# Another order of the steps in a talking-heads attention kernel with a local-attention gate

## The reference

```
s = talking_heads_attention(xn)      # 16 heads of 16; heads mixed before and after the softmax
g = silu(local_attention_stack(xn))  # 2 layers: window attention (8 heads of 64) and a GELU MLP
return x + s * g
```

## Time and profile before

| | |
|---|---|
| median of 3 runs | 5370.03 us (5368.29 to 5371.4) |
| the profiled execution, its own time | 5372.07 us |
| its span, first to last instruction | 5370.0 us |
| mean granted TensorE clock | 0.994 of full speed |
| busy: TensorE / VectorE / ScalarE / GpSimd | 95% / 69% / 50% / 49% |
| DMA | 52 GB/s over the span |

### The profile page before, as it was taken

How to read it: one execution, slowest core, us unless ns; L and a number is a source line. 1 busy time by engine, 2 the same in 40 slices (tenths; PEclk the granted TensorE clock), 3 DMA queues, 4 the chain that set the end, 5 groups by cost and what they waited for, 6 DMA issues and landing times. The chain is left out here.

```text
span 5370.0 us, 176617 instructions
## 1 busy us (share of the span) xinstructions
PE 5119.1 (95%) x72856; PEld 4155.2 (77%) x72856; DVE 3692.1 (69%) x8889; ACT 2659.8 (50%) x6551; POOL 2619.2 (49%) x2308
## 2 busy tenths in 40 slices
PE   6999999999999999999999999999999999999998
PEld 5887777877778777787777777777777777777776
DVE  6667676667766667666676666766667676676765
ACT  4445554455544454544545445454455544555544
POOL 4445554445544445444464444544445444454543
PEclk9999999999999999999999999999999999999999
DMA  2211111121111111111110111101111011111110
GB/s 79 95 66 63 46 35 64 45 67 42 38 61 56 57 41 38 61 61 53 40 64 35 61 53 51 58 31 61 54 50 58 30 61 62 42 58 39 52 49 17
DMA packets 51388, 280.78 MB, mean 52 GB/s; under 512 B 5280, under 2 KB 22688, under 8 KB 33696
## 3 DMA queue, kind: packets, MB, share of 16 engines
q1 hardware_dynamic: 39840, 252.69, 12.8%
q0 software_dynamic: 10752, 16.78, 1.7%
HBM read 249.01 MB, written 28.84 MB: 52 GB/s over the span
## 5 line engine op out<-in xcount | busy, mean ns | idle before, releaser
L1492 POOL TENSOR_TENSOR q_lo<-q_mix,q_hi 128x512 fp32r<-128x512 f32 x512 | 663.5, 1296 | 1349.7 <-ACT q_hi L979 1349.7
L992 ACT ACTIVATE probs<-bank_S,neg_max 128x512 f32<-128x512 f32 x1024 | 700.6, 685 | 1180.3 <-DVE neg_max L1220 993.7
L711 PE MATMUL bank_S<-k_hi,q_lo 128*128 128x512 f32 x2048 | 874.5, 427 | 9.6 <-POOL q_lo L1492 5.5
L1220 DVE TENSOR_REDUCE neg_max<-bank_S 128x1 f32<-128x512 f32 x1024 | 693.8, 684 | 263.5 <-PE bank_S L713 259.7
L713 PE MATMUL bank_S<-k_hi,q_hi 128*128 128x512 f32 x2048 | 803.9, 393 | 0.0
L712 PE MATMUL bank_S<-k_lo,q_hi 128*128 128x512 f32 x2048 | 803.5, 392 | 0.1
L728 PEld LDWEIGHTS bank_M<-mixer_n,probs 64*64 64x64 f32 x32768 | 534.1, 136 | 248.5 <-issue 161.3
L728 PE MATMUL bank_M<-mixer_n,probs 64*64 64x64 f32 x32768 | 606.1, 222 | 74.3 <-DVE mixer_n L1211 24.3
L1518 POOL TENSOR_TENSOR l_probs<-l_probs,l_inv 128x1024 f32<-128x1024 f32 (+1 forms) x256 | 428.8, 1682 | 491.7 <-DVE l_inv L1323 491.7
L1487 POOL TENSOR_TENSOR q_mix<-q_rope,w_pre 128x256 f32<-128x256 f32 x1024 | 637.6, 643 | 48.6 <-POOL q_lo L1492 1.8
L1042 ACT ACTIVATE l_probs<-l_probs,l_least 128x256 f32<-128x256 f32 (+1 forms) x1024 | 480.9, 471 | 253.0 <-DVE l_least L1303 252.6
...
## 6 DMA issues: line engine op xcount, KB each, us to landing
...
```

The source lines that it names most:

```text
L711: mm(bank[k][:], q_lo[q], k_hi[:, s, :], start=(s == 0), stop=False)
L992: fn(probs[:, n % PB, :], bank[k][:], ACT.Exp, bias=neg_max[:, n % 2:n % 2 + 1], accum_out=row_sum[:, n % 4:n % 4 + 1]).then_inc(emptied[k ...
L1220: v.tensor_reduce(neg_max[:, n % 2:n % 2 + 1], bank[k][:], AX.X, ALU.max, negate=True)\
L1492: g.tensor_tensor(q_lo[:, c % QB], q_mix[:], q_hi[:, c % QB].bitcast(F32), ALU.subtract)\
```

## The change

It replaces ORDER and LAST_ORDER by other permutations of the same steps, and swaps two neighbours in FIRST_ORDER. No step, instruction, buffer or DMA is added or removed. Two waits are added so that the new order is safe: talk_v on TensorE waits until both banks of x_turn.0 are taken out, and ScalarE's x_turn waits for all three talk projections to be filled. The number of times that consecutive TensorE steps use different tile shapes, counted over the whole of `program()` from the texts, is 1904 before and 1914 after. Of the two large texts, the lines that the next sections speak of:

```diff
 ORDER = """
...
-q_turn.0.1 qkv.0.3 part.4 mix.1 scores.5 q_turn.0.2 join.0.3 mixers.2 k_turn.0.2 scores.6 scores.7 expand.5 mix.2
-sigmoid.0 part.5 mixers.3 q_turn.0.3 k_turn.0.3 scores.8 scores.9 mix.3 local_scores.0.0 mixers.4 expand.6 part.6
-expand.7 sigmoid.1 weigh.0.0 values.0 local_scores.0.1 mix.4 part.7 expand.8 scores.10 scores.11 weigh.0.1 p_turn.0.0
-local_scores.0.2 part.8 mixers.5 expand.9 scores.12 scores.13 mix.5 local_scores.0.3 local_values.0.0 weigh.0.2
-mixers.6 scores.14 scores.15 mix.6 weigh.0.3 p_turn.0.1 sigmoid.2 part.9 silu scores.16 gated sigmoid.3 mixers.7
-p_turn.0.2 local_values.0.1 local_scores.0.4 expand.10 scores.17 scores.18 out_proj.0.0 mix.7 part.10 local_scores.0.5
-weigh.0.4 p_turn.0.3 local_values.0.2 values.1 mixers.8 local_scores.0.6 store local_values.0.3 p_turn.0.4 weigh.0.5
-scores.19 mix.8 local_scores.0.7 expand.11 out_proj.0.1 local_values.0.4 weigh.0.6 weigh.0.7 mixers.9 p_turn.0.5
-part.11 scores.20 expand.12 local_values.0.5 p_turn.0.6 part.12 mix.9 out_proj.0.2 expand.13 local_values.0.6
...
-part.18 scores.30 scores.31 expand.19 qkv.1.0 join.1.0 scores.32 mixers.15 qkv.1.1 q_turn.1.0 k_turn.1.0 part.19
-scores.33 join.1.1 scores.34 mix.15 mixers.16 qkv.1.2 k_turn.1.1 join.1.2 values.3 scores.35 expand.20 q_turn.1.1
...
-scores.45 scores.46 mix.21 local_scores.1.4 local_values.1.1 weigh.1.3 mixers.22 part.24 p_turn.1.2 weigh.1.4
-scores.47 local_scores.1.5 mix.22 expand.25 out_proj.1.0 scores.48 weigh.1.5 mixers.23 local_values.1.2 part.25
-p_turn.1.3 mix.23 local_scores.1.6 local_values.1.3 scores.49 p_turn.1.4 expand.26 mixers.24 part.26 scores.50
...
-part.27 scores.52 local_values.1.5 p_turn.1.6 scores.53 expand.28 mixers.25 part.28 out_proj.1.2 mix.25 p_turn.1.7
...
-scale up.1.2 scores.62 scores.63 mixers.31 x_turn.0 up.1.3 up.1.4 talk_q up.1.5 mix.31 talk_k down.1.0 down.1.1
-down.1.2 talk_v values.7 down.1.3 project.3
...
+mixers.1 expand.5 k_turn.0.1 qkv.0.3 mix.1 scores.5 scores.6 join.0.3 q_turn.0.2 part.5 k_turn.0.2 q_turn.0.3 expand.6
+sigmoid.0 k_turn.0.3 mixers.2 part.6 scores.7 local_scores.0.0 mix.2 mixers.3 weigh.0.0 scores.8 scores.9 expand.7
+mix.3 part.7 local_scores.0.1 p_turn.0.0 scores.10 weigh.0.1 mixers.4 values.0 sigmoid.1 expand.8 part.8
+local_values.0.0 scores.11 local_scores.0.2 mix.4 mixers.5 expand.9 scores.12 scores.13 p_turn.0.1 weigh.0.2 mix.5
+part.9 expand.10 silu sigmoid.2 scores.14 mixers.6 scores.15 gated local_values.0.1 sigmoid.3 p_turn.0.2 mixers.7
+part.10 scores.16 mix.6 expand.11 local_scores.0.3 scores.17 out_proj.0.0 mix.7 scores.18 weigh.0.3 local_scores.0.4
+values.1 mixers.8 local_values.0.2 weigh.0.4 p_turn.0.3 local_scores.0.5 part.11 local_values.0.3 p_turn.0.4 scores.19
+weigh.0.5 mix.8 expand.12 local_scores.0.6 part.12 mixers.9 out_proj.0.1 local_values.0.4 local_scores.0.7 mix.9
+weigh.0.6 expand.13 p_turn.0.5 scores.20 scores.21 local_values.0.5 p_turn.0.6 weigh.0.7 scores.22 part.13
...
+mixers.15 expand.19 down.0.0 down.0.1 down.0.2 down.0.3 mix.15 x_turn.1 scores.33 scores.34 mixers.16 qkv.1.0 join.1.0
+qkv.1.1 values.3 join.1.1 q_turn.1.0 part.19 k_turn.1.0 expand.20 qkv.1.2 part.20 mix.16 q_turn.1.1 expand.21
...
+scores.47 expand.25 out_proj.1.0 scores.48 weigh.1.4 mix.22 local_scores.1.5 local_values.1.2 mixers.23 p_turn.1.3
+part.25 scores.49 mix.23 local_scores.1.6 local_values.1.3 mixers.24 expand.26 part.26 expand.27 values.5 weigh.1.5
...
+scores.51 scores.52 part.28 local_values.1.5 p_turn.1.6 expand.29 weigh.1.7 mixers.25 scores.53 mix.25 mixers.26
+out_proj.1.2 part.29 local_values.1.6 p_turn.1.7 expand.30 scores.54 local_values.1.7 scores.55 mix.26 mixers.27
...
+up.1.0 mix.30 up.1.1 scores.62 scores.63 mixers.31 up.1.2 up.1.3 mix.31 x_turn.0 talk_v values.7 up.1.4 up.1.5 talk_q
+talk_k down.1.0 down.1.1 down.1.2 down.1.3 project.3
 FIRST_ORDER = """
...
-part.23 scores.44 p_turn.1.2 scores.45 expand.24 mix.21 local_scores.1.5 part.24 local_values.1.2 out_proj.1.0
+part.23 p_turn.1.2 scores.44 scores.45 expand.24 mix.21 local_scores.1.5 part.24 local_values.1.2 out_proj.1.0
...
 LAST_ORDER = """
...
-mixers.28 values.6 part.31 h_scale.1 scores.59 scores.60 mix.28 mixers.29 end.silu h_turn.1 scores.61 scores.62
-mixers.30 mix.29 up.1.0 up.1.1 up.1.2 up.1.3 up.1.4 up.1.5 scores.63 mix.30 down.1.0 down.1.1 down.1.2 mixers.31
-down.1.3 end.bound mix.31 end.gated end.sigmoid.0 end.sigmoid.1 end.sigmoid.2 end.sigmoid.3 values.7 project.3
-end.store
+h_scale.1 scores.59 expand.31 mix.28 mixers.29 h_turn.1 scores.60 part.31 scores.61 mix.29 up.1.0 up.1.1 up.1.2 up.1.3
+up.1.4 up.1.5 scores.62 down.1.0 mixers.30 end.silu down.1.1 down.1.2 down.1.3 end.bound scores.63 end.gated mix.30
+end.sigmoid.0 mixers.31 end.sigmoid.1 end.store mix.31 end.sigmoid.2 end.sigmoid.3 values.7 project.3
@@ -685,6 +684,8 @@
                     last.then_inc(filled[k], 1)
 
             def talk_v(step):
+                for c in range(KC):
+                    pe.wait_ge(emptied[f"F{c}"], now.fill(("x_turn", 0), f"F{c}"))
                 for t in range(TW):
                     k = f"S{t // 2}"
                     if t % 2 == 0:
@@ -949,7 +950,8 @@
 
                 if now.past(l):
                     act.wait_ge(filled["F2"], now.fill(("qkv", (l - 1) % LAYERS, TW - 1), "F2", ago=not l))
-                    act.wait_ge(filled["S1"], now.fill(("talk_v",), "S1", ago=not l))
+                    for kind in ("talk_q", "talk_k", "talk_v"):
+                        act.wait_ge(filled["S1"], now.fill((kind,), "S1", ago=not l))
                 for c in range(KC):
                     k = f"F{c}"
                     act.wait_ge(filled[k], now.fill(step, k))
```

More of the change, by code:

```diff
@@ L140 @@
-part.18 scores.30 scores.31 expand.19 qkv.1.0 join.1.0 scores.32 mixers.15 qkv.1.1 q_turn.1.0 k_turn.1.0 part.19
-scores.33 join.1.1 scores.34 mix.15 mixers.16 qkv.1.2 k_turn.1.1 join.1.2 values.3 scores.35 expand.20 q_turn.1.1
-mix.16 mixers.17 part.20 qkv.1.3 q_turn.1.2 k_turn.1.2 project.1 expand.21 join.1.3 scores.36 part.21 scores.37 mix.17
-scores.38 q_turn.1.3 expand.22 part.22 mixers.18 k_turn.1.3 scores.39 mix.18 local_scores.1.0 mixers.19 scores.40
-scores.41 mix.19 mixers.20 local_scores.1.1 weigh.1.0 expand.23 scores.42 part.23 values.4 local_scores.1.2 p_turn.1.0
@@ L145 @@
-scores.43 expand.24 weigh.1.1 weigh.1.2 scores.44 mix.20 local_scores.1.3 mixers.21 local_values.1.0 p_turn.1.1
-scores.45 scores.46 mix.21 local_scores.1.4 local_values.1.1 weigh.1.3 mixers.22 part.24 p_turn.1.2 weigh.1.4
-scores.47 local_scores.1.5 mix.22 expand.25 out_proj.1.0 scores.48 weigh.1.5 mixers.23 local_values.1.2 part.25
-p_turn.1.3 mix.23 local_scores.1.6 local_values.1.3 scores.49 p_turn.1.4 expand.26 mixers.24 part.26 scores.50
-out_proj.1.1 local_values.1.4 expand.27 values.5 local_scores.1.7 mix.24 weigh.1.6 weigh.1.7 p_turn.1.5 scores.51
@@ L155 @@
-down.1.2 talk_v values.7 down.1.3 project.3
+expand.0 part.0 expand.1 part.1 expand.2 bound qkv.0.0 join.0.0 scores.0 scores.1 part.2 qkv.0.1 mixers.0 k_turn.0.0
+q_turn.0.0 expand.3 join.0.1 scores.2 part.3 expand.4 qkv.0.2 mix.0 scores.3 scores.4 join.0.2 part.4 q_turn.0.1
+mixers.1 expand.5 k_turn.0.1 qkv.0.3 mix.1 scores.5 scores.6 join.0.3 q_turn.0.2 part.5 k_turn.0.2 q_turn.0.3 expand.6
+sigmoid.0 k_turn.0.3 mixers.2 part.6 scores.7 local_scores.0.0 mix.2 mixers.3 weigh.0.0 scores.8 scores.9 expand.7
@@ new lines @@
+weigh.0.5 mix.8 expand.12 local_scores.0.6 part.12 mixers.9 out_proj.0.1 local_values.0.4 local_scores.0.7 mix.9
+weigh.0.6 expand.13 p_turn.0.5 scores.20 scores.21 local_values.0.5 p_turn.0.6 weigh.0.7 scores.22 part.13
+out_proj.0.2 mixers.10 local_values.0.6 store p_turn.0.7 scores.23 local_values.0.7 project.0 out_proj.0.3 expand.14
+mix.10 half_turn.0 part.14 mixers.11 scores.24 mix.11 expand.15 shift_turn.0 scores.25 scores.26 values.2 mixers.12
+part.15 expand.16 h_scale.0 scores.27 scores.28 mixers.13 mix.12 h_turn.0 part.16 expand.17 scores.29 scores.30
@@ new lines @@
+mixers.14 mix.13 up.0.0 part.17 mix.14 up.0.1 up.0.2 up.0.3 up.0.4 up.0.5 expand.18 part.18 scores.31 scores.32
+mixers.15 expand.19 down.0.0 down.0.1 down.0.2 down.0.3 mix.15 x_turn.1 scores.33 scores.34 mixers.16 qkv.1.0 join.1.0
+qkv.1.1 values.3 join.1.1 q_turn.1.0 part.19 k_turn.1.0 expand.20 qkv.1.2 part.20 mix.16 q_turn.1.1 expand.21
+scores.35 join.1.2 k_turn.1.1 qkv.1.3 q_turn.1.2 project.1 mixers.17 k_turn.1.2 scores.36 join.1.3 part.21 scores.37
+mix.17 mixers.18 q_turn.1.3 expand.22 part.22 scores.38 k_turn.1.3 scores.39 mix.18 local_scores.1.0 expand.23
@@ new lines @@
+mixers.19 weigh.1.0 scores.40 scores.41 mix.19 local_scores.1.1 mixers.20 p_turn.1.0 scores.42 weigh.1.1 values.4
+part.23 local_values.1.0 local_scores.1.2 scores.43 mix.20 weigh.1.2 local_scores.1.3 expand.24 part.24 mixers.21
+p_turn.1.1 scores.44 scores.45 mix.21 local_scores.1.4 p_turn.1.2 weigh.1.3 local_values.1.1 mixers.22 scores.46
```

(38 more changed lines are left out.)

8 lines of the change are left out of this document (removed).

## The result

The changed kernel takes 5445.6 us (median of 4 runs, 5436.0 to 5454.6) against 5370.7 us: ratio 1.014, interval 1.0122 to 1.0158. It is slower by 75 us where 57 us less were forecast, and outside the range.

A forecast was written before the change was run, and what follows sets the result against it. TensorE was taken as the bound. Idle time falls 10.4 - 7.4 = 3.0 us a batch, 45 us over batches 1 to 15; with 12 us of clock and 0 for shape, 5370 - 57 = 5313 us, range 5245 to 5369.

The forecast's parts named there:

- slower rival: Added waits before talk_v and at the turns make the clock fall in each batch: 84 us more, 5397 us; chance 0.1.
- out_proj.0.0: Array's 3.00 us wait for VectorE's copy of local_values.0.1: gone; its slow clock stretches too, 12 us over the run.
- mix.6: Array's 0.97 us wait behind the multiplication of mixers.6, held beside weigh.0.2: gone, with three and more array steps between.
- mix.23: Array's 1.36 us wait for bank M1, whose copy stood behind a held mixers.23: gone.
- mix.2: Old 0.63 us wait at a rebuilt place; behind local_scores.0.0 a new wait of about 0.5 us for mixers.2.
- talk_v: New wait directly behind x_turn.0 until ScalarE and VectorE have taken both banks out: 1.9 us a batch.
- q_turn.0.3: New wait behind k_turn.0.2 for VectorE's join into the single buffer qk_tok: about 1.4 us a batch.
- k_turn.0.3: Wait for GpSimd's join at the rebuilt turns: 0.75 us with semaphores; the old wait there was 0.40.
- local_scores.0.0: New wait for VectorE's copy of k_turn.0.3, behind sigmoid.0: some 0.4 us a batch with semaphores.
- mix.25: Multiplication of mixers.25, now neighbour of weigh.1.7, held 1.9 us: wait of about 1.2 us, bounds 0 and 1.9.
- Unseen waits: Waits not visible by going through a text, because some queue is late: none to 4 us, 1.3 taken.
- Changes of shape: Tile shape changes between array steps, 0.09 us each, ten more: 1 us more; 0 in the sum, bounds -10 and +10.

The follow-up runs named there:

- e7: Changed kernel with its order untouched, SyncE's reloads of w_qkv_lo and w_1_lo issued when half_turn is filled, in all batches but the first; 5336.0 us.
- e1: Changed kernel with one step moved: store stands before scores.19 again instead of after local_values.0.6; 5301.4 us.
- e3: Changed kernel with one step moved: project.0 stands after scores.24 instead of after local_values.0.7, store stays late; 5406.2 us.
- e2: Old order with two steps moved as in the new one: store after local_values.0.6, project.0 after scores.22; 5520.6 us.
- e4: e1 with talk_v and values.7 exchanged, so that values.7 comes before talk_v; 5282.2 us.
- e6: Old order with one step moved: VectorE does sigmoid.3 after the copy of local_values.0.1 instead of before it; 5348.8 us.

## Why the prediction was wrong

**The sentence that failed** is the one on DMAs: "DMAs, on SyncE's and GpSimd's queues, move by less than a few us each and cover whole stages: 0." store moves from before local_values.0.3 to behind local_values.0.6, and project.0, whose addition overwrites what it reads, moves the other way, from behind scores.22, mix.10 and scores.23 to directly behind local_values.0.7. In the old kernel the addition runs 31 us after the store's issue; in the new one the array has ended project.0 4.8 us after it. At the old landing time of 6.2 us that would still have cost almost nothing, as e7 shows. What made it 8.8 us is that the store now starts within 3 us of two reloads. e1, e3 and e2 show the first half (the store is what project.0 waits for), e7 the second. So the term was put at 0 without comparing issue and use, and it measured 144 us. I went through the waits of TensorE's steps and of the turns, but not through `stored`, on which VectorE waits and TensorE only at one remove.

**The slower rival** had the right side and the wrong place. It let the clock fall at the clusters of new waits in each batch. At the turns it falls in 4 of 15 batches of e1, for 3.4 us each (in 9 in e3 and 7 in e4, at about the same waits); where it falls in each batch is mix.10. Its question, whether about 2 us do to the clock what 3.0 us did, is answered by e6 for a single wait: 1.84 us were followed by a slow stretch in 9 of 14 batches, 3.0 us in 8 of 14. So its mechanism is real, and only too rare at the turns to cost 84 us.

**The rest of the sum**, which e1 measures (5301 against 5313 forecast for it):
- out_proj.0.0: 43.0 us of idle time before L848 to 0.0 before L849. Right, and so is the slow clock there. (The prediction's 3.75 us for this out_proj are right, but the earlier trace rows show only its first three matmuls, 1.62 us.) But e6 shows that VectorE's queue was not the whole: the same cure in the old order returns more than half of it as a wait before p_turn.0.3. The new order escapes since gated comes sooner against the array's work: it ends 0.3 us behind out_proj.0.0 in e1, 4.0 us behind it in e6.
- mix.6, mix.23, values.0, local_values.0.5, mix.2, mix.22: none is over 0.1 us on average in e1. L729 has 29.0 us idle against 74.3 for L728; about 40 was forecast.
- talk_v: 1.6 us on average, 1.9 forecast. q_turn.0.3: 1.55, forecast 1.4. k_turn.0.3: 0.39, forecast 0.75. local_scores.0.0: 0.34 on average, forecast 0.4. mix.2: nothing, forecast 0.5.
- mix.25: 0.20 us, forecast 1.2. The neighbours weigh.1.7 and mixers.25 do collide, but less than was taken: the multiplication of mixers.25 takes 0.93 us on average in e1 (0.29 in the old kernel), where mixers.6 had taken 1.97.
- Unseen waits: forecast 1.3 us. k_turn.0.0 alone makes 1.2 on average, released by GpSimd's join: the new order has the key turn before its query turn. mix.11 and scores.16 add 0.3 each.
- The idle time of a batch is 7.8 us in e1, forecast 12.7 - 3.0 = 9.7. So these terms came out 2 us a batch better than forecast, from errors that partly cancel, while the clock gave back less: TensorE's busy time fell by 6 us where 12 were forecast. That e1 lands 12 us from the forecast is in part luck.
- Changes of shape: 1904 and 1914. No run isolates them. TensorE's busy time, 5113.0 us in e1 against 5119.1, gives no sign of a large cost. Where the prediction writes that this part gives nothing or 1 us back, its own ten extra changes make it 1 us of cost.

**Range and chances.** The range rested on waits of known kinds being larger or smaller. It had no case for one large wait that no list had, and 0.83 for faster was too sure for a change that moves every step past every other.
